# A state-space layer and a mixture of experts on one core: the four queues' order within a sequence period, delta's turn in another PSUM bank, and the residual in one VectorE pass

## The reference, cut to what matters

```python
def _forward(x, ...):                      # state-space layer
    xn = _layernorm(x, norm_w, norm_b)
    x_in, z = jnp.split(xn @ in_proj_w.T, 2, axis=-1)
    x_act = silu(conv(x_in, conv_w) + conv_b)
    x_ssm = x_act @ x_proj_w.T             # delta_s, B, C
    delta = softplus(delta_s @ dt_w.T + dt_b)
    # h = h * exp(-d_t) + b_t * u_t ;  y_t = h . c_t  for each token in turn
    return y * silu(z) @ out_proj_w.T + residual

x = x + _layernorm(_forward(_layernorm(x), ...))
# experts: softmax router, top 2, y = (silu(x W1) * (x W3)) W2, layernorm * gamma + beta
x = x + _layernorm(_ffn(_layernorm(x), ...))
```

## Time and profile before

| | |
|---|---|
| median of 3 runs | 1038.88 us (1036.8 to 1041.35) |
| the profiled execution: its own time | 1040.41 us |
| its span, first to last instruction | 1038.6 us |
| busy PE / PEld / DVE / ACT / POOL | 918.0 / 786.2 / 728.3 / 721.8 / 636.1 us |
| granted TensorE clock, mean | 0.955 of full |
| stage 1 up to its last `gated` | 0 to 536.8 us |
| router's end, slot table, stage 2's first row load | 536.8 to 580.4 us |
| stage 2 (143 expert tiles) | to 991 us |
| stage 3 | to the end |

### The profile page before, as it was taken

How to read it: one execution, slowest core, us unless ns; L and a number is a source line. 1 busy time by engine, 2 the same in 40 slices (tenths; PEclk the granted TensorE clock), 3 DMA queues, 4 the chain that set the end, 5 groups by cost and what they waited for, 6 DMA issues and landing times.

```text
span 1038.6 us, 25911 instructions
## 1 busy us (share of the span) xinstructions
PE 918.0 (88%) x6851; PEld 786.2 (76%) x6851; DVE 728.3 (70%) x2459; ACT 721.8 (69%) x1422; POOL 636.1 (61%) x820
## 2 busy tenths in 40 slices
PE   5999999999999999998842599999999999999955
PEld 2777777766777777777731599999999999999922
DVE  2379777889777888777773276776776777777746
ACT  3677787777877777766622477777777777787626
POOL 2344766677666777666646166666666666666647
PEclk9999999999999999999875699999999999999978
DMA  4001222021111011111066431111111111111075
GB/s 127 11 11 32 92 88 73 30 88 52 46 50 32 30 52 42 37 35 33 23 243 267 139 126 47 46 51 50 49 47 52 45 47 50 47 47 52 21 280 206
DMA packets 54157, 75.20 MB, mean 72 GB/s; under 512 B 11104, under 2 KB 32866, under 8 KB 53377
## 3 DMA queue, kind: packets, MB, share of 16 engines
q1 hardware_dynamic: 42784, 54.87, 16.8%
q0 software_dynamic: 8672, 16.93, 4.5%
q10 hardware_dynamic: 2560, 1.75, 0.5%
HBM read 47.09 MB, written 27.41 MB: 72 GB/s over the span
## 4 chain that ended last, share of the span: by engine, by line
PE 56%; DVE 21%; issue 11%; POOL 6%; ACT 2%; DMA 2%; SPq 1%; POOLq 0%; another core or an unknown queue 0%; DVEq 0%; ACTq 0%
PE pA L1701 11%; PE pR L1701 10%; PE pB L1709 5%; PE pY L1709 5%; PE pY L1559 4%; DVE y_both L1122 4%; PE pA L1445 3%; PE pY L1578 3%; PE pY L1595 3%; DVE placed L1253 2%; POOL chosen_scratch L646 2%; DVE y_both L1110 2%; PE pR L1587 2%; DVE y_both L1141 2%; DVE y_both L1134 2%
## 5 line engine op out<-in xcount | busy, mean ns | idle before, releaser
L646 POOL DMA_INDIRECT chosen_scratch<-yo,got_id x143 | 147.9, 1034 | 94.0 <-issue 88.2
L955 ACT ACTIVATE stage<-w_sb 128x1024 f32 x143 | 151.2, 1057 | 56.9 <-issue 56.9
L603 POOL DMA_INDIRECT slots_scratch<-xrow,send_at x128 | 139.4, 1089 | 37.6 <-issue 35.5
L1337 DVE TENSOR_TENSOR hidT<-pR,sil 128x512 f32<-128x512 f32 x143 | 98.9, 692 | 88.3 <-ACT sil L950 60.6
L1701 PE MATMUL pA<-xsT,stage 128*128 128x128 f32 x1144 | 153.0, 277 | 0.4 <-ACT xsT L939 0.4
L1701 PE MATMUL pR<-xsT,stage 128*128 128x128 f32 x1144 | 152.0, 276 | 0.0
L1701 PEld LDWEIGHTS pA<-xsT,stage 128*128 128x128 f32 x1144 | 140.9, 194 | 0.7 <-ACT xsT L939 0.7
L1701 PEld LDWEIGHTS pR<-xsT,stage 128*128 128x128 f32 x1144 | 140.0, 193 | 0.0
L1445 PE MATMUL pA<-xn,taps 128*128 128x512 f32 x256 | 128.2, 604 | 1.0 <-DVE taps L989 1.0
L636 POOL TENSOR_TENSOR ers<-eve,neg_half 128x1 f32<-128x1 f32 x143 | 81.5, 570 | 56.0 <-DVE eve L1349 41.8
L950 ACT ACTIVATE sil<-pA 128x512 f32<-128x512 f32 x143 | 85.2, 596 | 28.6 <-PE pA L1701 24.3
(11 more groups left out here) (191 smaller groups left out, 2101.7 us busy)
## 6 DMA issues: line engine op xcount, KB each, us to landing
got<-slots_scratch SPq DMA_DIRECT2D x143, 65.0 KB, 1.9
w_sb<-chosen_scratch SPq DMA_DIRECT2D x16, 512.0 KB, 5.3
w_sb<-in_w_dram SPq DMA_DIRECT2D x1, 6144.0 KB
xin<-in_x_dram SPq DMA_DIRECT2D x16, 256.0 KB
xr<-in_x_dram SPq DMA_DIRECT2D x16, 256.0 KB
x_scratch<-x SPq DMA_DIRECT2D x16, 256.0 KB
w_sb<-in_w_dram SPq DMA_DIRECT2D x4, 1024.0 KB
fx<-x_scratch SPq DMA_DIRECT2D x1, 4096.0 KB
```

The lines of the kernel that those rows point to most:

```text
L603: eng.indirect_dma_start(slots_d, bass.IndirectOffsetOnAxis(ap=send_at[:, s % 2, k, t:t + 1], axis=0), xrow[:, s % 2, k, t, :], None).then ...
L646: eng.indirect_dma_start(chosen_d, bass.IndirectOffsetOnAxis(ap=got_id[:, j % NGOT:j % NGOT + 1], axis=0), yo[:, q, :], None, bounds_check ...
L955: eng.activation(stage[:, j % NSTAGE, :, :].rearrange("p k f -> p (k f)"), w13_sb[:, bass.ds(e, 1), :, :].rearrange("p o k f -> p (o k f)" ...
L1337: eng.tensor_tensor(hidT[:, p, :], pR[:, p, :], sil[:, p, :], ALU.mult).then_inc(hid_ready, 1)
```

## The change

`DEPTH` grows from 6 to 7: one more round. All four `unit` lists are written anew, so that a sequence's steps on an engine stand about a quarter period from where they stood, relative to the steps of its neighbours. `delta_turn` writes pA bank 1, the second bank of the convolution, in place of pR bank 0, and waits for the second `conv_out` of its sequence; `decay` reads it there; `project_gate` 0 of the next sequence waits for that read. `x1_norm` and its tile are gone, `residual` is one scalar_tensor_tensor per 128 columns on VectorE (at × rs3 + xr); the shift term, constant along a row, is left out of x1 there and kept per sequence in `shift3[:, s, :]`, and stage 3 adds it to `fshift` in one more small GpSimd addition per part. `diagonal` and `odd` name waits on the y chain of the sequence before. On SP `store_x1(14)` stands behind `load_early`. In the diff below the first `residual` and `unit` are GpSimd's, `x1_norm` is ScalarE's, the second `residual` VectorE's, and the last two pieces are `project_gate` and `delta_turn` on TensorE.

```diff
-DEPTH = 6
+DEPTH = 7
...
+        shift3 = sb("shift3", [P, NS, NT4])
...
-            def residual(s):
-                need(eng, x1n_ready, s, 1, 1)
-                need(eng, xf_ready, s, 2, 1, ago=1)
-                need(eng, x1_stored, s, 16, 16, ago=1)
-                eng.tensor_tensor(x1[:, :, :], x1n[:, :, :], xr[:, :, :], ALU.add).then_inc(x1_ready, 1)
...
             def unit(q):
-                send(q[6], 0)
-                send(q[6], 1)
...
+                send(q[7], 0)
+                send(q[7], 1)
+                carry(q[4], 4)
+                send(q[7], 2)
+                carry(q[4], 8)
+                rstd_1(q[1])
+                send(q[7], 3)
+                join(q[4], 8)
+                token(q[5])
+                carry(q[3], 1)
...
-                eng.wait_ge(f_rstd, 2 * h + 1)
+                eng.wait_ge(f_rstd, 3 * h + 1)
                 eng.tensor_tensor(fshift[:, h % 2, c], fnm[:, h % 2, c], frs[:, h % 2, c], ALU.mult).then_inc(f_rstd, 1)
+                eng.wait_ge(shift3_ready, g + n)
+                eng.wait_ge(f_rstd, 3 * h + 2)
+                eng.tensor_tensor(fshift[:, h % 2, c], fshift[:, h % 2, c], shift3[:, g:g + n, :].rearrange("p g t -> p (g t)"), ALU.add).then_inc(f_rstd, 1)
...
-                    i = eng.activation(dec1[:, s % 2, f, :], pR[:, 0, :], ACT.Tanh, scale=ndtw[:, f:f + 1], bias=ndtb[:, f:f + 1])
+                    i = eng.activation(dec1[:, s % 2, f, :], pA[:, 1, :], ACT.Tanh, scale=ndtw[:, f:f + 1], bias=ndtb[:, f:f + 1])
...
-            def x1_norm(s):
...
+            def residual(s):
+                need(eng, rstd3, s, 1, 1)
+                need(eng, at_ready, s, 1, 1)
+                need(eng, xf_ready, s, 2, 1, ago=1)
+                need(eng, x1_stored, s, 16, 16, ago=1)
+                for t in range(NT4):
+                    i = eng.scalar_tensor_tensor(out=x1[:, t, :], in0=at[:, t, :], scalar=rs3[:, t:t + 1], in1=xr[:, t, :], op0=ALU.mult, op1=ALU.add)
+                i.then_inc(x1_ready, 1)
...
                 if f == 0:
-                    need(eng, u_ready, s, 2, 2, ago=1)
+                    need(eng, dec1_ready, s, 2, 1, ago=1)
...
-                need(eng, ht_ready, s, 2, 1, ago=1)
+                need(eng, u_ready, s, 2, 2)
                 for t in range(NT4):
-                    i = eng.transpose(pR[:, 0, tile(t)], xs[:, s % 2, t, 0:1].broadcast_to([P, P]), ident[:, :])
+                    i = eng.transpose(pA[:, 1, tile(t)], xs[:, s % 2, t, 0:1].broadcast_to([P, P]), ident[:, :])
```

More of the change, by code:

```diff
@@ new lines, in unit @@
+                gather(q[5], 4)
+                fold(q[5], 2)
+                gather(q[5], 2)
+                fold(q[5], 1)
+                gather(q[5], 1)
+                mask(q[4], 2)
+                mask(q[4], 4)
+                odd(q[4])
+                decayed(q[5])
+                logits(q[6])
+                with_diagonal(q[5])
+                largest(q[6])
+                diagonal(q[4])
+                where(q[6])
+                margin(q[6])
+                choose(q[6])
@@ L1299, in _ @@
+                gated(q[5])
+                positions(q[6])
+                shift_1(q[1])
+                stats_1(q[0])
+                dots(q[3])
+                aggr_1(q[0])
+                attend(q[5])
+                stats_3(q[5])
+                aggr_3(q[5])
+                scan(q[4], 0)
+                var_3(q[5])
+                scan(q[4], 1)
+                residual(q[5])
+                expand(q[3], 0)
             run_units(NS, NS + DEPTH, unit)
@@ new lines, in unit @@
+                conv(q[3], 0, 1)
+                rank(q[7])
+                r16_turn(q[5], 1)
+                level(q[5], 8)
+                next_b(q[4])
+                project_out(q[6])
+                level(q[5], 4)
+                states(q[5], 0)
+                project_gate(q[3], 0)
+                states(q[5], 1)
+                conv(q[3], 0, 2)
+                h_turn(q[5], 0)
+                conv(q[3], 0, 3)
+                h_turn(q[5], 1)
+                from_state(q[5], 0)
```

213 lines of the change are left out of this document (77 added, 136 removed).

## The result

The changed kernel takes **991.99 us** (median of 4 runs, 991.05 to 993.33) where the kernel before took 1039.05 beside it: ratio 0.9548, 95% interval 0.9523 to 0.9572. The profiled execution took 992.59 us, its span is 990.4.

What follows compares the result with a forecast made beforehand. A loop between VectorE and TensorE bounded the old first stage; TensorE's queue would bound the new. Last `fold` 8 −49.7, drain −2.1, last stage +2.0 sum to −49.8: profiled 990.6, median 989 us, range 979 to 1008.

Steps and rivals of the forecast that it cites:

- the last two gaps: Last two first-stage gaps between `fold` 8 starts: no new sequence to convolve, so the VectorE-TensorE loop bounds, 25.1 us each.
- the last stage: Nine parts each get another GpSimd addition of 0.20 us and a 0.08 wait; seven on the chain, +2.0 us.
- the drain: After the last `fold` 8: residual follows the last rstd_3 at once and takes 1.1 us, −2.1 us.
- The period: First stage, per sequence: TensorE's 27.6 us plus 0.3 for wide/narrow matmul changes and 0.5 for waits, 28.4 instead of 31.6.
- rival A: First stage: TensorE's queue bounds, floor 27.6 us, period 28.0 to 28.9, 984 to 995 us; the forecast, chance 0.56.
- rival B: First stage: VectorE and GpSimd lock each other, losing 3.4 to 5 us a period, 996 to 1018 us; chance 0.28.
- whoever issues first holds the path: VectorE and GpSimd's shared SBUF interface: an exclusive lock, held by the first issuer for its whole instruction; no separate size.
- What made the old loop long: First stage: VectorE's order put other sequences' steps ahead of `diagonal`; gram 8 waited 16.8 us in ten periods; loop 31.64 us.
- `placed`: VectorE, first stage: 2.06 us in a steady period beside GpSimd's `carry`, expected near 0.3 us after the change.
- Residual: First stage: four 128x128 instructions add 1.1 us to VectorE; ScalarE loses 1.6 us, GpSimd 1.26 us.
- Start: First sequence: its `fold` 8 at 58.1 instead of 54.25 us, +3.9, with the h = 4 copy queued later on ScalarE.
- Delta's turn and `token`: First stage: bank move costs nothing, gate 0 covered by 8 us; `token`'s wait for GpSimd's last send costs nothing, bound 1 us.

Runs made afterwards that it cites:

- next_b early: Changed kernel with next_b on TensorE moved from behind level 8 to right behind delta_turn: ratio 0.9494.
- the third addition: Run without it: changed kernel lacking the added GpSimd addition of the kept mean term in the last stage, computation incomplete: ratio 0.9474.

## Why the prediction was right, and where it was not

Predicted 989 us, measured 991.99. The sum of the terms was −49.8 and the spans show −48.2. That closeness is partly luck: the last two gaps missed by 6.2 us, and the middle gaps (2.3), the last stage (1.9), the expert tiles (0.7) and the drain (0.5) paid most of it back.

**The period: right size, half the reason.** 28.4 was predicted and 28.21 measured over twelve gaps. TensorE's own need was put at 27.6; the early periods, and most periods of the kernels with carry 2 held back and no tap left out, show 27.42, all of it busy. That rival A's floor exists is shown. But the changed kernel runs at it in only three of its middle gaps. In most of the others the chain leaves TensorE for VectorE and GpSimd, and what lengthens it is rival B's mechanism at a smaller size: residual beside carry 2, which B named, 1.04 us. `decayed` takes 1.93 in place of 1.22 as well. B asked for 3.4 to 5 us of losses, and VectorE's busy time fell by 1.8 when the meeting was undone. So the 0.8 us that the forecast put on top of the floor for transitions and waits were not what it said; the 0.8 measured are, in the main, one lock: transitions cost nothing (27.42 is below even the 27.6 of the pitches), and without the lock the waits cost nothing either. The prediction also took from its rule that whoever issues first holds the path, and said that the trace agrees. The rows agree that one of the two stands still until the other has ended. But `placed` starts 0.60 us ahead of the carry and is the one that stands, and `residual` starts 0.2 us ahead of carry 2 and stands, so the recorded starts don't tell who goes first.

**What made the old loop long: right.** It was `diagonal` behind `margin`, `choose`, `gated` and `positions`; moving it back behind three of the four costs the whole gain. The prediction's account of it, a loop of two queues with gram 8 waiting, is what that experiment showed: at the full clock the gap with the step moved back is 29.99 us in two of six cases and 30.3 on average, where the terms 24.9, 1.8 and 2.8 give 29.5. The two things missing from it are `margin`, 0.9 us in that loop beside GpSimd and 0.15 in the changed kernel, and the lower granted clock behind TensorE's wait.

**`placed`: right.** It takes 0.28 us now, 2.06 before.

**Residual: the price right, the place not.** 1.14 us on VectorE by itself, as costed (1.1), as the earlier trace rows said. The half rate for two non-bf16 SBUF sources that the Trainium skill states (Vector Engine (DVE) Microarchitecture Reference, section 7) does not show in this row either. It was costed as if alone, though, and beside carry 2 it took 2.18.

**Start: right**, 58.53 against 58.1, and the first gap 26.6 against 26.2.

**The last two gaps: the step that failed.** "The loop is, at 24.9 to 25.1": 56.4 us in place of 50.2. The sum dropped a term of its own. The prediction had put `project_out` into this loop, at 1.8 us, and got 26.7; for the last gaps it went back to the loop without it. `project_out` stands in the trace of these gaps (16 matmuls, 1.95 us at 455.34, with carry 2 held back). With 26.7 the two gaps would have been put at 53.4, and 3.0 of the 6.2 us would be left.

Part of those 3.0 goes with the clock. TensorE stood idle for `diagonal`, the granted clock of the last gap is 0.82, and the second profile of the same kernel, at 0.94, has 54.7 for the two, though not all of the 1.7 us need be the clock's. The lock's part is not shown. With carry 2 held back the two gaps are 52.7, but without the third addition, whose first stage has no such wait, they are 52.2. The halves of the loop missed in opposite ways. In the last gap of the kernel with carry 2 held back, 27.03 us at a clock of 0.87, VectorE's half takes 11.85 us (438.86 to 450.71), summed to 10.0 from the pitches of before, 0.7 of the difference being `decayed` beside a carry. TensorE's takes 15.2, where 14.9 and `project_out` made 16.7.

**Drain: right**, −2.6 against −2.1. **Delta's turn and `token`: right**, no cost in the period: TensorE sat idle for 2.5 us in all before the 64 gate matmuls of the changed kernel, none of it for the decay, and GpSimd's wait for its last send (1.4 us a period, above the bound of 1) is slack, as moving it showed. Whether the new order holds with delta's turn in its old bank was not run.

**Last stage: wrong by its size.** "Seven additions of 0.28, +2.0": the kernel without it is 0.4 us shorter there. The term counted the addition and not what the addition moves.

**The range.** Its low end of 979 doesn't follow from its own terms: 12 or 14 periods of 27.8 and a start of −1 take 12 to 13 us off 989, which is 976 to 977. The result doesn't hang on it.

**The residual's worth.** The prediction booked the move as a small cost against the order's gain. The runs show that neither stands alone: instructions without order 1.0078, order without the one-pass residual 0.9776, both 0.955.

The version that beats both is the changed kernel with carry 2 held back for the first expand: 976.15 us, ratio 0.9436, 1.1% below the changed kernel's 0.9539 to 0.9548.

## What to carry to other kernels

Where the rows show two engines holding each other up, a schedule is not only a list of durations: look at each two-input VectorE instruction for the GpSimd instruction beside it, and put a wait on the one that has time, so that it runs beside something that it doesn't meet. When a queue waits for another engine, a long wait behind the waiting instruction isn't a second cost until the chain passes through it; look at the granted clock of the periods first. When a loop has been summed with a new term, use that sum in every stretch where the loop bounds. And a bound that is reached at the end of a change (TensorE at 27.42) can have the next one 0.1 us below it, so try one thing less before working on it.

## What the hardware showed that was not expected

- A VectorE subtraction of 4 values took 2.66 us, until two GpSimd instructions in a row had ended: it got no turn between them. A cast of 8 values with one SBUF input took 3.09 in the same place. The reverse is seen too: carry 2 took 2.09 instead of 1.30 us where `residual` was first.
- One program kept its slow rhythm (28.55 us) through both of its profiles and a second one with the same first stage left it after three gaps. In both, and with next_b early, the length of a gap goes with whether carry 2 starts 0.80 us or more, or 0.71 us or less, behind `residual`.
- GpSimd's indirect transfers did not go out for free beside bulk loads: 5.93 us without an issue in a stretch with a DMA share of 0.98. That the loads are the cause is not shown.
- TensorE, idle for 2.3 us ahead of gram 8 with `diagonal` moved back, ran at half its full clock for the 3 us behind it in some periods (31.6 us) and not in others (29.99).
- In periods of 28.5 us VectorE's `dots` and ScalarE's copy of level 8 start 1.3 to 1.4 us after the modelled end of the matmuls that they wait for; in periods of 27.4 the copy starts 0.5 us after it or less. Moving next_b took this wait out of VectorE's queue; what delays it stays open.
